# Second cross-attention of a two-layer gated network: value products moved to the end of a step, and ScalarE and VectorE exchange their transposes' copies

## What is computed

```python
q = proj(query, Wq, bq)          # 8 x 16 heads x 112 x 16
k = proj(key, Wk, bk)            # 8 x 16 heads x 375 x 16
v = proj(value, Wv, bv)
attn = jnp.einsum('bhqd,bhkd->bhqk', q, k) / jnp.sqrt(jnp.float32(Dh))
attn = jax.nn.softmax(attn, axis=-1)
out = jnp.einsum('bhqk,bhkd->bhqd', attn, v)
out = out.transpose(0, 2, 1, 3).reshape(B, -1, D)
out = jnp.einsum('bsd,ed->bse', out, Wo) + bo
```

## Time and profile before

| | |
|---|---|
| median of three runs | 749.33 us (747.06 to 749.74) |
| profiled execution, span from first to last instruction | 755.5 us |
| profiled execution, its own time | not listed beside the span |
| TensorE busy | 719.0 us, 95% |
| VectorE busy | 530.6 us, 70% |
| ScalarE busy | 446.3 us, 59% |
| GpSimd busy | 194.8 us, 26% |
| mean granted TensorE clock | 0.993 of 2.4 GHz |

### The profile page before, as it was taken

How to read it: one execution, slowest core, us unless ns; L and a number is a source line. 1 busy time by engine, 2 the same in 40 slices (tenths; PEclk the granted TensorE clock), 3 DMA queues, 4 the chain that set the end, 5 groups by cost and what they waited for, 6 DMA issues and landing times.

```text
span 755.5 us, 15906 instructions
## 1 busy us (share of the span) xinstructions
PE 719.0 (95%) x5594; PEld 589.5 (78%) x5594; DVE 530.6 (70%) x1266; ACT 446.3 (59%) x1203; POOL 194.8 (26%) x317
## 2 busy tenths in 40 slices
PE   9999999999998995999999999989999999899998
PEld 8567777777776874899999996756776667789988
DVE  3788788788676320487777866748788897798754
ACT  3676667766757411577777754577888788121231
POOL 4132220322000062011100107644555437311000
PEclk9999999999999997999999999999999999999999
DMA  5322333422110576377765524430000000000001
GB/s 167 103 81 61 79 96 114 117 82 79 41 43 11 167 237 209 129 235 263 238 211 194 204 85 125 130 128 1 2 3 2 2 2 1 1 1 1 1 7 43
DMA packets 43537, 69.81 MB, mean 92 GB/s; under 512 B 6611, under 2 KB 35036, under 8 KB 43204
## 3 DMA queue, kind: packets, MB, share of 16 engines
q1 hardware_dynamic: 41924, 65.14, 27.7%
q0 software_dynamic: 1536, 3.67, 1.6%
HBM read 52.56 MB, written 8.26 MB: 80 GB/s over the span
## 4 chain that ended last, share of the span: by engine, by line
PE 78%; DVE 9%; ACT 5%; issue 4%; DMA 2%; another core or an unknown queue 2%; SPq 1%; POOL 0%; ACTq 0%; DVEq 0%; POOLq 0%
PE ps L1528 11%; PE ps L1796 10%; PE ps L1813 8%; PE ps L2015 7%; PE ps L1590 5%; PE ps L1593 5%; PE ps L1897 4%; PE ps L1632 3%; PE ps L1841 3%; PE ps L1720 3%; PE ps L1652 3%; PE ps L1851 3%; PE ps L2050 2%; PE ps L1603 2%
## 5 line engine op out<-in xcount | busy, mean ns | idle before, releaser
L1528 PE MATMUL ps<-ident,arena 112*122 112x112 f32 (+5 forms) x584 | 81.6, 274 | 5.9 <-ACT rt L862 3.8
L1528 PEld LDWEIGHTS ps<-ident,arena 112*122 112x122 f32 (+5 forms) x584 | 63.5, 154 | 29.5 <-issue 14.7
L1032 DVE TENSOR_REDUCE negmax<-ps 112x1 f32<-112x375 f32 x128 | 61.2, 541 | 31.0 <-PE ps L1897 30.9
L818 ACT ACTIVATE arena_r<-ps,bt 128x128 fp32r<-128x128 f32 x168 | 70.0, 418 | 17.8 <-PE ps L1796 17.8
L1796 PE MATMUL ps<-OT,arena 128*128 128x128 f32 x672 | 78.5, 275 | 0.6 <-issue 0.6
L2015 PE MATMUL ps<-arena_r 128*112 128x384 f32 x384 | 75.8, 345 | 1.9 <-DVE acc L1317 1.0
L1796 PEld LDWEIGHTS ps<-OT,arena 128*128 128x128 f32 x672 | 76.7, 192 | 0.9 <-issue 0.8
L819 ACT ACTIVATE OT<-ps,bt 128x128 f32<-128x128 f32 x168 | 71.1, 425 | 0.0
L2015 PEld LDWEIGHTS ps<-arena_r 128*112 128x112 f32 x384 | 63.8, 175 | 4.0 <-DVE arena L1450 1.2
L1027 DVE TENSOR_REDUCE negmax<-ps 112x1 f32<-112x487 f32 x64 | 39.5, 658 | 22.7 <-PE ps L1632 22.7
L677 ACT ACTIVATE arena<-ps,negmax 112x487 f32<-112x487 f32 x64 | 42.8, 672 | 16.1 <-DVE negmax L1027 16.1
(11 more groups left out here) (312 smaller groups left out, 1704.4 us busy)
## 6 DMA issues: line engine op xcount, KB each, us to landing
arena<-in_up_w SPq DMA_DIRECT2D x21, 1024.0 KB, 4.9
arena<-in_down_w SPq DMA_DIRECT2D x8, 1024.0 KB
arena<-arena SPq DMA_DIRECT2D x128, 60.9 KB, 2.0
arena<-in_wqkv SPq DMA_DIRECT2D x1, 3072.0 KB, 10.1
arena<-in_ctx SPq DMA_DIRECT2D x8, 375.0 KB
slot_rows<-acc SPq DMA_DIRECT2D x6, 448.0 KB, 3.5
OT<-slot_rows SPq DMA_DIRECT2D x21, 128.0 KB, 3.0
slot_out<-yo SPq DMA_DIRECT2D x21, 128.0 KB, 2.7
```

The lines of the kernel that those rows point to most:

```text
L818: act.activation(he_hi[:, i % 2, m, :], src, ACT.Gelu, bias=bt[:, i % 3, m:m + 1])
L1032: dve.tensor_reduce(negmax[0:TQ, h % 4:h % 4 + 1], ps[0:TQ, S_BANKS[h % 4], 0:TK], AX, ALU.max, negate=True)\
L1528: return pe.transpose(dst, src, ident[0:k, 0:k])
```

## The change

TensorE's value products, and the transposes of the inverses behind them, go from the middle of a step to its end, just ahead of the next step's scores. ScalarE now copies T0 and T1, ahead of its four exponentials, and VectorE copies T2 and T3, behind its four maxima. The two semaphores of the copies change places with that.

```diff
--- before.py
+++ after.py
@@ -256,7 +256,7 @@
         s_ksw = [sem("l0_k_swapped_even"), sem("l0_k_swapped_odd")]
         L1 = ring("l1", "q qe s max exp pt pv ote")
         s_qt = sem("l1_q_biased")
-        s_pta, s_ptv = sem("l1_pT_heads_2_3_ready"), sem("l1_pT_heads_0_1_ready")
+        s_pta, s_ptv = sem("l1_pT_heads_0_1_ready"), sem("l1_pT_heads_2_3_ready")
         s_rall, s_rw1, s_rT = sem("l1_sums_inverted"), sem("l1_inverses_spread"), sem("l1_inverses_transposed")
         s_rTe = sem("l1_inversesT_ready")
         s_res1, s_stat1, s_rstd1, s_sq1, s_glog, s_glogd = (sem("l1_rows_" + n) for n in (
@@ -895,6 +895,9 @@
 
             def l1_step(n, v):
                 g = n * H1 + 4 * v
+                if g:
+                    l1_pt(g - 4)
+                    l1_pt(g - 3)
                 l1_exp(n, 4 * v)
                 l1_exp(n, 4 * v + 1)
                 l1_exp(n, 4 * v + 2)
@@ -903,9 +906,6 @@
                 l1_exp(n, 4 * v + 3)
                 if g == 0:
                     v_out(B - 1)
-                if g:
-                    l1_pt(g - 2)
-                    l1_pt(g - 1)
                 if n >= 2 and v == 0:
                     l1_x(n - 2)
                 if n and v == 3:
@@ -917,9 +917,9 @@
             for n in range(B):
                 for v in range(H1 // 4):
                     l1_step(n, v)
+            l1_pt(8 * H1 - 4)
+            l1_pt(8 * H1 - 3)
             l1_x(6)
-            l1_pt(8 * H1 - 2)
-            l1_pt(8 * H1 - 1)
             for i in range(9, 16):
                 w_high(i)
             l1_norm(7)
@@ -1403,8 +1403,8 @@
                 l1_max(n, 4 * v + 2)
                 l1_max(n, 4 * v + 3)
                 if g:
-                    l1_pt(g - 4)
-                    l1_pt(g - 3)
+                    l1_pt(g - 2)
+                    l1_pt(g - 1)
                 if n == 0 and v == 1:
                     l1_q(1, 1)
                 if n and v == 0:
@@ -1425,8 +1425,8 @@
             for n in range(B):
                 for v in range(H1 // 4):
                     l1_step(n, v)
-            l1_pt(8 * H1 - 4)
-            l1_pt(8 * H1 - 3)
+            l1_pt(8 * H1 - 2)
+            l1_pt(8 * H1 - 1)
             l1_sums(7)
 
 
@@ -1906,9 +1906,9 @@
             def l1_pt(g, h):
                 pe.wait_ge(L1["exp"], g + 1)
                 if g % 4 >= 2:
-                    pe.wait_ge(s_ptv, g // 4 * 2 + g % 2 + 1)
+                    pe.wait_ge(s_pta, g // 4 * 2 + g % 2 + 1)
                 elif g >= 4:
-                    pe.wait_ge(s_pta, g // 4 * 2 - 1 + g % 2)
+                    pe.wait_ge(s_ptv, g // 4 * 2 - 1 + g % 2)
                 if g == 0:
                     pe.wait_ge(s_kve, 4 * B)
                 for j in range(3):
@@ -1980,14 +1980,8 @@
                     l1_pt(g - 3, (g - 3) % H1)
                 if n >= 2 and v == 1:
                     l1_g(n - 2)
-                if v >= 2:
-                    l1_pv(n, v - 2)
-                elif n:
-                    l1_pv(n - 1, v + 2)
                 if n >= 2 and v == 0:
                     l1_x(n - 2)
-                if n and v == 1:
-                    l1_rT(n - 1)
                 if n == 0 and v == 1:
                     l1_q(1)
                 if n and v == 2:
@@ -1997,6 +1991,12 @@
                 if g:
                     l1_pt(g - 2, (g - 2) % H1)
                     l1_pt(g - 1, (g - 1) % H1)
+                if v >= 2:
+                    l1_pv(n, v - 2)
+                elif n:
+                    l1_pv(n - 1, v + 2)
+                if n and v == 1:
+                    l1_rT(n - 1)
 
             for n in range(B):
                 for v in range(H1 // 4):
```

## The result

The changed kernel takes 754.51 us in the median of four runs (753.43 to 756.61), the kernel before 749.54 on the same chip (747.06 to 750.36). **The medians differ by 5.0 us.** The ratio on record is 1.008 with a 95% interval of 1.0056 to 1.0104; it is not the quotient of the two medians (1.0066) and stands for 6.0 us. The forecast was 7.9 us slower.

What follows compares the result with a forecast made beforehand. A loop through VectorE was taken to set the 4.28 us interval; a new ScalarE loop of 0.83 + 0.62 + 0.76 + 2.38 = 4.59 us over 30 intervals adds 7.9 to 749.33, giving 757.2 us, range 753.0 to 762.0.

Steps and rivals of the forecast that it cites:

- The loop through VectorE: Second cross-attention, kernel before: T2 waits for VectorE's copy of T0 behind four maxima, setting a 4.29 us interval.
- Step 1: TensorE: value products at the step's end take 0 to 0.17 us less work, if a tiling change goes away.
- Step 2: ScalarE: copies ahead of exponentials close a new loop from scores to scores, 4.59 us against 4.28.
- The upper end of the range: Whole copies of 0.87 us and every hand-over 0.05 more: interval 4.75 us, sum +12.7 us.
- the 6.2 us that it takes off the span: Whole kernel: median runs lie 6.2 us below the profiled span of 755.5, a difference assumed to stay.
- Step 3: VectorE: its copies of T2 and T3 start where copies did before and cost nothing; cover over 1.5 us.
- Step 4: Inverses' product behind value products costs nothing; 0.7 us of slack in the maxima also absorbs 1.4 us of long intervals.
- step 5: ScalarE's other work fits in 1.50 us of idle; one last-batch step has more, some tenths, left out.
- Step 6: End of the stage: last scores to the transposition of row block 6 stay about 5.3 us, no gain or loss.
- A (drains): TensorE: adjacent tiled products save 0.17 us of drain a step, 742.8 us, faster; chance 0.05.
- B (no difference): Second cross-attention: the new loop is hidden, interval 4.28 to 4.35, 747.9 to 750 us; chance 0.09.
- C: Late inverses delay maxima and exponentials, up to 764.2 us, or TensorE is granted less clock; slower still, chance 0.06.

Runs made afterwards that it cites:

- experiment 1: Kernel before with only TensorE's half of the change (value products and inverses' transposes last in a step), copies as before: 796.88 us, ratio 1.0553.
- experiment 4: Kernel before with the value products moved the other way, directly behind the same step's scores: 757.86 us, ratio 1.0001.
- experiment 2: Kernel before with only the copies exchanged between ScalarE and VectorE, TensorE's order as before: 769.81 us, ratio 1.0147.
- Experiment 8: Kernel before with ScalarE copying T0 ahead of its exponentials and T3 behind them, VectorE T1 and T2 behind its maxima: 756.52 us, ratio 0.9995.
- experiment 3: Changed kernel with ScalarE's two copies behind the first exponential instead of ahead of it: 770.40 us, ratio 1.0173 to the kernel before.
- experiment 6: Changed kernel with T2 and T3 transposed twice in the steps with least TensorE work: 763.29 us, ratio 1.0089 to the kernel before.
- experiment 11: Changed kernel's TensorE order, but only T0 copied ahead of ScalarE's exponentials: 760.74 us, ratio 1.0169 to the kernel before.
- experiment 7: Kernel with only the copies exchanged, plus T2 and T3 transposed twice in steps with least TensorE work: 765.36 us, ratio 1.0134.

## Why the prediction was right, point by point

**What bounds the kernel before: right.** The loop through VectorE explains experiment 1 (5.00 = 4.29 + 0.71) and experiment 4 (T0 later by 0.7 and nothing changes).

**Step 1, value products at the end: right in sign, its bound settled.** Taken as 0 to 0.17 us less TensorE work; it is 0, since the 0.17 is paid in front of scores as well (experiment 1) and the 0.54 behind scores in front of products as well (experiment 4). Alone it costs 40 us. This half only works with the other: it takes the filler out of T2's old wait, and the exchange of copies takes that wait away. What the prediction lacks is its use: it brings T2 and T3 forward, and with them VectorE's copies (experiment 2).

**Step 2, the new loop: right, with one term mis-sized.** Forecast 0.83 + 0.62 + 0.76 + 2.38 = 4.59. Measured in the plain step: 0.83 (529.94 to 530.77), 0.62 (to 531.39), **0.68** (to 532.07), 2.38 (to 534.45), together 4.51. The wrong term is "two copies until ScalarE's next instruction". I took 533.12 to 533.88 as a start-to-start distance of free-running copies. But the second copy there was waiting for T3: T2 starts at 532.53, and T2 and T3 end 0.97 later, at 533.50. The pair lasts 0.87 there and 0.79 here, and one copy 0.45, so the second started 0.42 behind the first there and 0.34 here. Experiment 8 shows 0.35 for a single copy (503.41 to 503.76). 0.08 x 30 = 2.4 us. Sixteen intervals are longer than 4.51 by 0.02 or more and give 0.9 back: 7.9 - 2.4 + 0.9 = 6.4, and the trace has 6.4. Seven of them, 4.57 or 4.58, end at the first scores of a sequence, which also wait for its spread queries (2.45 instead of 2.38 from the first exponential; what costs the 0.07 isn't shown), the seven behind these have 0.02 to 0.03 more, one has 0.05, and the last 0.20. The difference to the measured 5.0 and 6.8 is within their intervals (4.2 to 7.8, 5.8 to 9.8).

The upper end of the range was worked out for one hand-over 0.05 longer, though the text says every one; the 6.2 us that it takes off the span are set right in the section on the result, and their place in the sum did no harm, since the median was the starting point.

**Step 3, VectorE's copies of T2 and T3 cost nothing: right.** In the plain step they end at t = 3.88, and the next T0 starts at 5.34 without a wait: a cover of 1.5 us, and still 1.05 in the last interval.

**Step 4, late inverses and stretched intervals: right but for the last interval.** VectorE waits eight times, 3.5 us, for the transposed inverses, and six of the seven intervals behind them are plain. Every fourth interval is longer, which was to be the sign against this step, but by 0.07 at most, and it is not the one with the inverses. The 1.4 us of long intervals went into the slack of the late exponentials, down to 0.2 us in the last interval, 4.71:

```profile
620.44 0.39 DVE L1394 COPY rinvT<-ps 128x224 f32<-128x224 f32 x1 [0.38 <-PE ps L1528]
...
621.43 0.90 DVE L1371 SCALAR_TENSOR_TENSOR acc<-acc 112x64 f32<-112x64 f32 x1
...
622.06 0.79 ACT L869 ACTIVATE arena<-ps 125x336 f32<-125x336 f32 x2 [0.67 <-PE ps L1528]
...
622.36 1.91 DVE L1032 TENSOR_REDUCE negmax<-ps 112x1 f32<-112x375 f32 x4
...
622.95 0.57 ACT L862 ACTIVATE arena<-ps,negmax 112x375 f32<-112x375 f32 x1
```

The scores of this step start at 620.62. VectorE has waited 0.38 for the inverses and then has gate arithmetic, so its maxima start at t = 1.74 instead of 0.92, and the first exponential at 2.33 instead of 2.13. ScalarE's copies are on time, so step 5's guess, a ScalarE with more work than fits, is not what made this interval longer.

**Step 6, the end: right within 0.15 us.** Last scores to the transposition: 625.33 to 630.56, 5.23 against 5.38.

**The rivals.** A (drains) fell in experiments 1 and 4. B (no difference) fell. Of C the first half, the chain behind the inverses, came out in one step of seven, for the 0.2 us above; its second half, TensorE granted less clock, is absent from both profiles of the changed kernel but there in those of experiments 1, 2, 3, 6 and 11. I had given it a word and no price; in experiment 1 I estimate it at 16 of 40 us. That the idle is its cause is argued: it came with more idle, but the filling of experiments 6 and 7 doesn't prove it, and behind the last scores of experiment 4, with plain intervals of 4.28, the clock was 0.84 from 629 to 640 us.

**What the profile would show:** T2 with hardly any wait, the first exponential behind two copies (at t = 2.13, forecast 2.2), scores waiting for ScalarE: all there. Wrong was that VectorE would wait longer for scores than 30.9 us; it is 28.4, because it now also waits 3.8 us for transposes and 3.5 for inverses.

## What to carry to other kernels

When an instruction is moved ahead on an engine, follow the loop that it joins, not the wait that it removes: here a wait of up to 0.6 us on TensorE was traded for 0.68 us of copies in front of four exponentials that the next step's scores need. Two edits that are 40 us and about 12 us slower alone (ratios 1.055 and 1.015) were 5 to 7 us slower together, so halves of such a change are no measure of the whole. Part of the first two numbers is clock. Before a start-to-start distance goes into a sum, ask whether the second instruction was waiting in that row.

## What was not expected of the hardware

- TensorE's granted clock answered to small edits inside the stage. With 5.0 us intervals and 1 us of idle in each it was 0.83 to 0.91 on average from 500 to 660 us, so often at the lower of its levels (1.2 of 2.4 GHz). With plain intervals of 4.51 to 4.58 us it fell for a few steps in four profiles (the lowest are 0.68 from 534 to 546 us and 0.57 from 579 to 583 us, both in experiment 2) and not in three others. At low clock the 24 value products of experiment 1 took 1.35 us instead of 0.78.
- Executions of one kernel on one chip spread with it: the kernel before had 745.9 us at a mean clock of 1.000 and 751.4 at 0.993. Stage differences of 1 us and less, plain in the profile, drown in that.
- The weight load behind scores comes 0.54 us late in front of value products, and the one behind value products 0.17 us late in front of scores, the same as in front of full-width transposes.
